# Column filter of a wavelet encoder: full-height array tiles replaced by two row groups of four lane blocks

## What is computed

```
def _swt2_level3(a):                     # a: normalised image 0
    for dil in (1, 2):
        a = _circ(_circ(a, DEC_LO, dil, 1), DEC_LO, dil, 2)
    aL, aH = _circ(a, DEC_LO, 4, 1), _circ(a, DEC_HI, 4, 1)
    return _circ(aL, DEC_LO, 4, 2), _circ(aL, DEC_HI, 4, 2), _circ(aH, DEC_LO, 4, 2), _circ(aH, DEC_HI, 4, 2)
cA, cH, cV, cD = _swt2_level3(x[0])
...
dmt = jnp.concatenate([low_att, high_att], axis=1)      # 4 sub-bands, scaled by channel attention
out = jax.nn.leaky_relu(conv3x3(dmt, W_enc, b_enc), 0.01)
return out + conv3x3(x, W_id, b_id)
```

## Time and profile before

| | us |
|---|---|
| runs of the kernel before, median of 3 | 1796.16 |
| the profiled execution, its own time | 1792.46 |
| its span, first to last instruction | 1790.7 |

### The profile page before, as it was taken

How to read it: one execution, slowest core, us unless ns; L and a number is a source line. 1 busy time by engine, 2 the same in 40 slices (tenths; PEclk the granted TensorE clock), 3 DMA queues, 4 the chain that set the end, 5 groups by cost and what they waited for, 6 DMA issues and landing times.

```text
span 1790.7 us, 69361 instructions
## 1 busy us (share of the span) xinstructions
PE 1753.9 (98%) x31540; PEld 1506.5 (84%) x31540; DVE 1377.6 (77%) x1807; ACT 1288.0 (72%) x1395; POOL 665.7 (37%) x449
## 2 busy tenths in 40 slices
PE   9999999999999999989999999999999999999997
PEld 9997999999999999975879888667877868996676
DVE  5665577777877877768788788888788887887875
ACT  5554666666666666667878787787878878787884
POOL 0005788888888888744003003011030030030000
PEclk9999999999999999999999999999999999999999
DMA  9884399888888888547999999999999999999994
GB/s 188 244 291 142 108 256 247 207 208 217 211 216 217 214 214 216 140 110 179 249 228 239 235 252 236 234 249 230 242 231 255 239 227 241 241 245 225 251 238 138
DMA packets 132966, 391.86 MB, mean 219 GB/s; under 512 B 49884, under 2 KB 50656, under 8 KB 118464
## 3 DMA queue, kind: packets, MB, share of 16 engines
q1 hardware_dynamic: 132672, 387.43, 83.7%
HBM read 258.88 MB, written 128.45 MB: 216 GB/s over the span
## 4 chain that ended last, share of the span: by engine, by line
PE 52%; ACT 1%; issue 1%; DVE 1%; POOL 0%; DVEq 0%
PE ps L1791 52%; ACT pool_of L1614 0%; DVE pool_of L1621 0%; DVE ps L2001 0%; POOL big L1396 0%; DVE tail L1980 0%; ACT big L1166 0%; ACT pool_of L1908 0%; ACT big L1892 0%; ACT big L1900 0%; ACT big L1179 0%; ACT pool_of L1608 0%; ACT ps L1635 0%; ACT ps L1929 0%; DVE tail L1994 0%
## 5 line engine op out<-in xcount | busy, mean ns | idle before, releaser
L1791 PE MATMUL ps<-big,tail 64*64 64x448 f16 x3840 | 331.1, 349 | 4.1 <-DVE ps L2001 1.2
L1791 PE MATMUL ps<-pool_of 64*64 64x448 f16 x5184 | 310.6, 352 | 10.5 <-DVE pool_of L1627 4.2
L1791 PE MATMUL ps<-big,pool_of 64*64 64x448 f16 x3552 | 306.2, 350 | 4.5 <-issue 3.7
L1791 PE MATMUL ps<-pool_of,tail 64*64 64x448 f16 x4896 | 304.0, 349 | 2.6 <-issue 2.6
L1292 DVE BATCH_NORM_STATS2 pool_of<-big 128x6 f32<-128x448 f32 x392 | 232.3, 616 | 78.5 <-DMA big<-in_x 78.4
L1791 PEld LDWEIGHTS ps<-pool_of 64*64 64x64 f16 x5184 | 219.9, 107 | 61.6 <-issue 10.7
L1791 PEld LDWEIGHTS ps<-pool_of,tail 64*64 64x64 f16 x4896 | 202.7, 106 | 53.6 <-issue 3.3
L1066 PE MATMUL ps<-pool_of 112*128 112x246 f16 x1344 | 218.8, 271 | 3.4 <-DVE pool_of L1280 1.4
L1070 PE MATMUL ps<-pool_of 112*128 112x168 f16 x1344 | 217.8, 243 | 0.0
L1791 PEld LDWEIGHTS ps<-big,tail 64*64 64x64 f16 x3840 | 182.4, 106 | 41.7 <-issue 3.9
L1791 PEld LDWEIGHTS ps<-big,pool_of 64*64 64x64 f16 x3552 | 174.5, 106 | 43.6 <-issue 6.6
(11 more groups left out here) (254 smaller groups left out, 3940.0 us busy)
## 6 DMA issues: line engine op xcount, KB each, us to landing
out<-tail SPq DMA_DIRECT2D x448, 224.0 KB, 3.6
big<-in_x SPq DMA_DIRECT2D x392, 224.0 KB, 5.2
pool_of<-in_x SPq DMA_DIRECT2D x139, 560.0 KB, 7.5
tail<-in_x SPq DMA_DIRECT2D x69, 560.0 KB, 7.7
pool_of<-row_filtered SPq DMA_DIRECT2D x110, 224.0 KB, 4.0
row_filtered<-big SPq DMA_DIRECT2D x2, 6272.0 KB, 22.8
pool_of<-in_x SPq DMA_DIRECT2D x30, 392.0 KB, 7.9
row_filtered<-big SPq DMA_DIRECT2D x4, 1568.0 KB, 9.1
```

The costliest lines, as they stand in the source:

```text
L1791: mm = pe.matmul(psum[bank + r][C * k:C * k + C, 0:NT], wt[i % 2][lanes, h, s, kx, :], v[u][lanes, rows_of(k), kx:kx + W], start=False, st ...
```

## The change

The 224 input columns are cut into four blocks of 56 instead of two halves of 112. Two blocks lie in lanes 0 to 55, two in lanes 64 to 119 (`LANES` is 120), so that a product with the lower lanes uses array rows 0 to 63 and one with the upper lanes rows 64 to 127. Lane 56 holds the additive part: a row of DRAM with minus the mean times the sum of the filter taps, and `fw` has a row of column sums for it; `shifted_rows` and its operations go away. The output columns are laid out as two halves of 28 (`HT`), each in a PSUM bank of its own; each lane block meets only the part of the columns where the matrix isn't zero.

```
-    fw = fw.reshape(H, 2 * VW)
+    fw = fw.reshape(H, 2 * NI, 2, HT).transpose(0, 2, 1, 3).reshape(H, 2 * VW)
+    blocks = np.zeros((2, BLK + 1, 2, 2 * VW))
+    blocks[:, :BLK] = np.roll(fw, 4, axis=0).reshape(2, 2, BLK, 2 * VW).transpose(1, 2, 0, 3)
+    blocks[0, BLK] = fw.sum(axis=0)
...
-                for sw in range(2):
-                    o = psum[banks_of(tile) + sw][:, 0:VW]
-                    for k, (a, b) in enumerate(((0, 0), (0, 1), (1, 0))):
-                        v = fw[:, 1, b, sw * VW:sw * VW + VW]
-                        pe.matmul(tiles(o)[:, :, 15:NTILE], lhs[:, 1, a, :], tiles(v)[:, :, 15:NTILE], start=(k == 0), stop=False)
...
+                for k in range(3):
+                    product(down, 0, k, 0, 0, HT, k == 0, False)
+                    product(up, 1, k, 1, 0, HT // 2, k == 0, False)
+                    mm = product(up, 0, k, 1, HT // 2, HT // 2, False, False)
+                mm.then_inc(half_done, 1)
+                pe.wait_ge(half_done, tile + 1)
+                for k in range(3):
+                    product(up, 0, k, 0, 0, HT // 2, False, False)
+                    product(down, 1, k, 1, 0, HT, False, k == 2)
+                    mm = product(up, 1, k, 0, HT // 2, HT // 2, False, k == 2)
                 mm.then_inc(gen_done, 1)
...
-                act.copy(d[slot][:, 0, r, :, :], ps[:, q:q + 2, 0:VW]).then_inc(hi_done, 1)
+                act.copy(in_halves(d[slot][:, 0, r, :, :]), of_banks(q)).then_inc(hi_done, 1)
...
-                dve.tensor_tensor(d[slot][:, 1, r, :, :], ps[:, q:q + 2, 0:VW], d[slot][:, 0, r, :, :], ALU.subtract)\
+                dve.tensor_tensor(in_halves(d[slot][:, 1, r, :, :]), of_banks(q), in_halves(d[slot][:, 0, r, :, :]), ALU.subtract).then_inc(lo_done, 1)
...
+            return v.rearrange("p s (i b t) -> p b (s i) t", b=2, t=HT)          # in_halves
+            return ps[:, q:q + 2, 0:VW].rearrange("p b (m t) -> p b m t", t=HT)  # of_banks
...
+            for h in range(2):
+                sp.dma_start(scratch[h, 0, BLK:BLK + 1, :, :], level.rearrange("a s c -> a (s c)").unsqueeze(1).broadcast_to((1, H, P))).then_inc(level_out, 16)
...
-            shifted_rows(pool, halo, bias_row).then_inc(normal, 1)
...
-                    shifted_rows(pool, v, bias_row).then_inc(s_ready, 1)
```

More of the change, by code:

```diff
@@ L455, in write @@
                     first = FIRST
[L456 to L459, removed]
+                    for j, w, p, n in pieces(wc):
+                        sp.dma_start(scratch[j // 2, j % 2, p:p + n, 0:FIRST, :].rearrange("w r e -> w (r e)"),
+                                     rows[hh][w:w + n, 0:FIRST, :, :].rearrange("w r s c -> w (r s c)")).then_inc(rows_first, 16)
+                for j, w, p, n in pieces(wc):
+                    sp.dma_start(scratch[j // 2, j % 2, p:p + n, HR * hh + first:HR * hh + HR, :].rearrange("w r e -> w (r e)"),
+                                 rows[hh][w:w + n, first:HR, :, :].rearrange("w r s c -> w (r s c)")).then_inc(rows_out[hh], 16)
             sp.dma_start(fh[:, :, :], t["fh"]).then_inc(fh_in, 16)
@@ L505, in sync @@
                 sp.wait_ge(first_split, 2 + u)
[L506 to L508 removed]
+                for g, n in ((0, BLK + 1), (1, BLK)):
+                    sp.dma_start(s_in[u][64 * g:64 * g + n, :, :, :].rearrange("w h r e -> w h (r e)"), block_rows(scratch, g, n, CH * (u + 2) + 1, CH))\
                       .then_inc(step_in[u], 16)
@@ L936, in encoder @@
         gen_done = sem(top, "gen_done")
+        half_done = sem(top, "half_done")
         hi_done = sem(top, "hi_done")
@@ L1055, in gen, with product @@
                     pe.wait_ge(lo_done, tile - 1)
-                for sw in range(2):
-                    def tiles(v):
-                        return v.rearrange("p (i t) -> p i t", i=NI)
-                    def both(v):
-                        return tiles(v)[:, :, 2:NTILE].rearrange("p i (h t) -> p i h t", h=2)[:, :, :, 13:27]
-                    o = psum[banks_of(tile) + sw][:, 0:VW]
-                    for k, (a, b) in enumerate(((0, 0), (0, 1), (1, 0))):
-                        v = fw[:, 1, b, sw * VW:sw * VW + VW]
-                        pe.matmul(tiles(o)[:, :, 15:NTILE], lhs[:, 1, a, :], tiles(v)[:, :, 15:NTILE], start=(k == 0), stop=False)
-                    for k, (a, b) in enumerate(((0, 0), (0, 1), (1, 0))):
-                        v = fw[:, 0, b, sw * VW:sw * VW + VW]
-                        pe.matmul(tiles(o)[:, :, 0:15], lhs[:, 0, a, :], tiles(v)[:, :, 0:15], start=False, stop=False)
-                        mm = pe.matmul(both(o), lhs[:, 0, a, :], both(v), start=False, stop=(k == 2))
+                q = banks_of(tile)
+                up, down = slice(0, BLK + 1), slice(64, LANES)
+                def product(lanes, h, k, half, first, count, start, stop):
+                    a, b = ((0, 0), (0, 1), (1, 0))[k]
+                    o, v = [m.rearrange("p (m t) -> p m t", t=HT)[:, :, first:first + count]
+                            for m in (psum[q + half][:, 0:VW], fw[lanes, h, b, half * VW:half * VW + VW])]
+                    return pe.matmul(o, lhs[lanes, h, a, :], v, start=start, stop=stop)
+                for k in range(3):
[8 more added lines that the diff above has]
+                    mm = product(up, 1, k, 0, HT // 2, HT // 2, False, k == 2)
                 mm.then_inc(gen_done, 1)
```

125 lines of the change are left out of this document (62 added, 63 removed).

## The result

The changed kernel takes **1938.8 us** (median of 4 runs, 1935.2 to 1941.3); the kernel before took 1796.4 beside it (4 runs). The ratio is 1.0786, 95% interval 1.0754 to 1.0819: slower by 7.9%. Forecast were 1762 us and "faster"; the time lies 161 us above 1778, the end of the forecast's own range, and 150 above 1789, up to where its first rival was to hold. The profiled execution has a span of 1937.1 us.

A forecast was written before the change was run, and what follows sets the result against it. PE was taken to bound the kernel, with DVE next in the encoder. 24.5 steps at 1.23 us gave 30.1, other tiles 4: 34 us off 1792.5 is 1758.5, or 1762 on the median's footing; range 1744 to 1778.

The forecast's parts named there:

- its first rival: Encoder filter: PE's tile hardly shrinks (1.38 us) or the DMA pause stays; 1783 to 1796 us; chance 0.10.
- the one on DMA: Encoder loads: 4.59 MB a step at 254 GB/s is 18.1 us, fitting a 20.4 us step; at most 1 us a step.
- The smaller term that failed: Before the encoder: many smaller writes and two tiny DVE operations, hidden behind PE's row filter, within 1 us.
- The products: Column filter on PE: row groups overlap, 480 ns a half, 0.23 us wait between halves; tile 1.19 us against 1.385.
- rows that take turns: Rival in the filter's products: row groups do not overlap, tile 2.05 us, 1944 us in all; chance 0.06.
- weight loads in line: Rival in the filter's products: 98 ns loads cannot run under products, tile 2.37 us, 2016 us; chance 0.02.
- DVE and the copies: Encoder stage: DVE's 1.31 us a tile limits it to 9.93 us instead of 11.16; runs of 28 cost nothing.
- The clock: Rival: a slower kernel through a granted clock lowered by the short waits; chance 0.02.
- Additive part: Before the encoder: its two DMAs stand in SP's queue ahead of the first unit load; 4 us allowed.
- POOL: Loses a 2.36 us operation twice a step, some 120 us in all; counted as nothing, since PE does not wait.
- convolutions: Encoder's convolution stages after each filter stage: still 10.5 us.
- images part: The part with 64 x 64 tiles: as long as before.

The follow-up runs named there:

- the transfers alone: No computation kept: single transfers of various lane counts, each waited for, some writes issued together; writes of 14336 B a lane took 10.59 us at 57 lanes, 4.39 at 56.
- the run without chunks: The changed kernel, 57-lane loads kept, without the loads of the statistics' chunks after the first four (statistics wrong): 1791.3 us, 0.9977 of the kernel before.
- the transfers mended: The changed kernel with a one-row scratch of 224 lanes and unit loads of 56 and 56 lanes plus a 4 KB row; three versions: 1774.0, 1772.2, 1771.0 us.
- the 1774 us kernel: The changed kernel with a one-row scratch written in 112, 96, 12 and 4 lanes, and loads of 56, 56 and a 4 KB row: 1774.0 us, 0.9877.

## Why the prediction was wrong

*The step that failed* is the one on DMA, "I cost it at nothing, at most 1 us a step". It counted bytes: 4.59 MB a step at 254 GB/s. That rate was a row of 16 engines at work (DMA share 1.03 there), and the change left only three of them to half of the units' bytes. It cost 123 us in the encoder (695 against 572) and 12 before it. I had looked for lane counts in the shapes of PE and POOL, and read those of the DMAs, 57, 56, 52 and 4, only as sizes.

*The smaller term that failed* is "the many smaller writes ... hidden behind PE's row filter, within 1 us": 30 us. The cover was there only while a write took 20 us; at 36 (the same pieces in the transfers alone) the next part of the filter needs the buffer first.

*The products.* Right, and a little better than forecast. The rate of 1/2.4 ns a column stands in the trace of the kernel before, at a clock of 1.00: products of 224 columns, two side by side (L1100), begin after 96 ns at the same place, those of 448, four side by side (L1791), after 190 (medians), so 224 columns more take 94 ns, 0.42 each. Starts of products in a stage without waits (us): the second half of a tile, the first half of the next, and after `half_done` the second half of that one:

```
upper rows, 336 columns  253.096 253.249 253.391 | 253.534 253.676 253.819 |         254.215
lower rows, 168 columns  253.093 253.177 253.253 | 253.549 253.620 253.696 |         254.212
                         253.325 253.401 253.474 | 253.769 253.844 253.917 |
```

The two row groups run side by side, and one product of 168 columns follows another after about 75 ns, not 80. From half to half a tile takes 254.212 - 253.093 = 1.12 us, not 1.19. At `half_done` no product begins for 0.295 us, 0.22 more than between two others: as forecast. The rivals of rows that take turns (1944 us) and of weight loads in line (2016) are out, though the first came within 5.2 us of the time: a number that fits shows no cause. Against the second, the loads last 94 ns, and products follow at 75 in the same rows.

*DVE and the copies.* The undisturbed stage, and its products by form:

```profile
252.41 9.57 PE L1082 MATMUL ps<-pool_of 56*128 56x336 f16 x144
262.07 2.17 PE L1123 MATMUL ps<-d_odd,shared 128*64 128x224 f16 x41
```

```profile
L1082 PE MATMUL ps<-pool_of 57*128 57x168 f16 x96 | 9.1, 234 | 0.5
L1082 PE MATMUL ps<-pool_of 56*128 56x336 f16 x48 | 8.8, 305 | 0.0
```

From its start to the convolution's the stage is 9.66 us, forecast 9.93. Eight tiles of 1.12 are 9.0; of the other 0.7, 0.43 a stage are waits for DVE's remainder, as the prediction said. That is read in the run without chunks, 11.6 us in 27 stages:

```profile
PEld ps L1080 <- DVE d_odd L1301: 6.0, 27, 0.6
PEld ps L1080 <- DVE pool_of L1301: 5.6, 27, 0.3
```

Runs of 28 columns cost nothing (before, 0.84 to 0.86 us for the remainder and 0.72 for the copy):

```profile
L1303 DVE TENSOR_TENSOR pool_of<-ps,pool_of 128x672 f16<-128x672 f32 x104 | 88.0, 846 | 14.1 <-ACT pool_of L1175 14.1
...
L1175 ACT CAST pool_of<-ps 128x672 f16<-128x672 f32 x104 | 74.3, 716 | 99.4 <-PE ps L1082 99.3
```

*The clock.* The chances give 0.02 to a slower kernel by the clock, lowered by the short waits. They do not lower it: without chunks it is 1.00 over 546 us with all 224 of these waits. It fell to 0.51 where PE had idled for 2.42 and 1.05 us, so it nearly doubled the loss (61 us of busy time beside 70 of idle time) and did not begin it.

*Additive part, POOL, convolutions, images part.* As forecast: nothing, nothing, 10.44 to 10.60 us, and from the last filter product to the end 1022 to 1028 us (before 1021.5).

With the transfers mended the time is 1771 to 1774 us, inside the forecast's own range, for another DMA layout than the one that was to be judged, and in part by luck. The gain is 22 to 25 us, forecast 34. The filter alone gave more than forecast: without chunks the encoder is 45 us shorter than before. In the profiled execution of the 1774 us kernel, 17 us shorter than the one before, 18 of the 45 go with the chunks, 4 with the later start and some 6 after the encoder.

## What to carry to other kernels

When a change alters the lanes of a tensor, read each DMA's lane count, factor it, and cost the transfer on the engines that it then gets (here 57 lanes had 3 and took 10.59 us, 56 had 14 and took 4.39); after it, cost whatever else has to pass the same engines. Bytes against a measured rate hold only for transfers of the shape that was measured (254 GB/s in the earlier trace rows, 76 for the 57 lanes alone). Where an engine waits for DMA while the DMA share is low, as at 0.28 here, count the packets under way: three at a time is a shape, not a bandwidth.

## What the runs showed that was not expected

- One lane more made a transfer 2.4 times (writes, 10.59 against 4.39 us) and 3 times (loads, 4.39 against 1.47 us) as long.
- Four lanes of 57344 B take 8.97 us, as twelve do; 112 take 20.06.
- Splitting a write of 112 lanes into 52+56+4 takes 36.4 us, into 48+4+48+8+4 44.7.
- With 112 lanes written at once the encoder started at 177.3 us again, but the three filter stages beside the last writes took 39.6 us, as with 96, 12 and 4 lanes (39.3), one of them 18.0.
